# Local transformers on 32-query blocks: values stationary in 64x64 tiles, probabilities divided in SBUF by DVE, mask laid by products of 64 rows, values moved tile by tile

## The reference, cut to what matters

```python
WINDOW, HEADS, DIM_HEAD, DEPTH = 32, 16, 64, 6
x = shift_tokens(x)                      # channels 64.. come from the token before
q, k, v = split(x @ Wqkv)                # 16 heads of 64
q = rotary(l2norm(q) * qs); k = rotary(l2norm(k) * ksc)
sim  = einsum('bhwie,bhwje->bhwij', bq, bk2) * 8.0   # bq: blocks of 32 queries,
                                                     # bk2: the 32 keys before and the 32 own
sim  = where((i < j) | (i > j + 32) | (j == -1), -max, sim)
out  = einsum('bhwij,bhwje->bhwie', softmax(sim), bv2)
x    = x + out @ Wo
h    = layernorm(shift_tokens(x)) @ W1 + b1          # then a * gelu(gate) @ W2 + b2, added to x
```

## Time and profile before

| | |
|---|---|
| median of 3 runs | 4340.34 us (4339.49 to 4340.35) |
| span of the profiled execution | 4339.8 us |
| first local transformer, first projection to end | from about 505 us to 2145 us |
| one iteration in the steady stretch | 32.65 us (1502.14 to 1534.79) |
| iterations in the two local transformers | 2 x 48 and their tails |
| mean granted TensorE clock | 0.957, in the steady stretch 1.00 |

### The profile page before, as it was taken

One profiled execution on the slowest core, in us unless ns is written; L12 is line 12 of the kernel. 1 busy time (PEld: TensorE's weight loads), 2 busy tenths in 40 slices (PEclk: granted clock), 3 DMA queues, 4 the chain that ended last, 5 costly groups with the idle time before them and its releaser, 6 DMA issues. The chain is left out here.

```text
span 4339.8 us, 130231 instructions
## 1 busy us (share of the span) xinstructions
PE 3995.2 (92%) x46283; PEld 2655.5 (61%) x46283; DVE 3715.0 (86%) x12505; ACT 3380.3 (78%) x10657; POOL 3380.2 (78%) x4196
## 2 busy tenths in 40 slices
PE   6888799999999999999767999999999999996686
PEld 2333357767767767766553677767776776763464
DVE  6999789999999999999476999999999999974646
ACT  5888489999999999999414999999999999983122
POOL 3999698888888888888296888888888888861313
PEclk7999899999999999999897999999999999997887
DMA  1000101111111111111002111111111111100000
GB/s 28 1 1 1 46 24 31 41 31 36 41 27 49 31 34 44 26 34 27 15 1 53 31 27 41 36 41 31 36 41 27 51 29 29 37 24 3 6 3 10
DMA packets 78571, 122.04 MB, mean 28 GB/s; under 512 B 26024, under 2 KB 47204, under 8 KB 77924
## 3 DMA queue, kind: packets, MB, share of 16 engines
q1 hardware_dynamic: 77924, 113.71, 10.3%
HBM read 35.56 MB, written 1.05 MB: 8 GB/s over the span
## 5 line engine op out<-in xcount | busy, mean ns | idle before, releaser
L1095 POOL TENSOR_TENSOR local_qk<-local_qk,local_rb 128x512 f32<-128x512 f32 x768 | 975.7, 1271 | 224.2 <-DVE local_rb L1485 210.1
L1365 ACT ACTIVATE local_pr<-local_tb,local_nmax 128x96 f32<-128x96 f32 x3072 | 995.0, 362 | 68.7 <-DVE local_nmax L1501 67.1
L1191 PE MATMUL local_pj<-local_wqkv,local_xs 128*128 128x512 f32 x1536 | 808.4, 619 | 31.8 <-DVE local_rb L1485 17.8
L1101 POOL TENSOR_TENSOR local_qk<-local_qk,local_rinv 128x512 f32<-128x512 f32 x768 | 786.6, 1045 | 7.5
L1501 DVE CUSTOM_DVE_ANT_0 local_tb<-local_tb,local_mask 128x96 f32<-128x96 f32 x3072 | 689.2, 290 | 46.5 <-PE local_tb L1213 43.7
L1365 ACT ACTIVATION_READ_ACCUMULATOR local_pr<-local_tb,local_nmax 128x1 f32 x3072 | 703.3, 229 | 0.0
L1117 POOL TENSOR_TENSOR local_pr<-local_pr,local_rsum 128x384 f32<-128x384 f32 x768 | 622.4, 826 | 36.5 <-DVE local_rsum L1507 36.5
L1482 DVE TENSOR_TENSOR local_qk<-local_pj,local_rope 128x512 f32<-128x512 f32 x768 | 523.6, 682 | 62.8 <-ACT local_sq L1348 44.1
L1348 ACT ACTIVATE local_sq<-local_pj 128x512 f32<-128x512 f32 x768 | 462.2, 627 | 123.3 <-PE local_pj L1191 119.0
L1485 DVE TENSOR_TENSOR local_rb<-local_pj,local_rope 128x512 f32<-128x512 f32 x768 | 523.2, 681 | 2.8 <-POOL local_qk L1095 2.8
L1492 DVE TENSOR_REDUCE local_ss<-local_sq 128x8 f32<-128x512 f32 x768 | 512.0, 678 | 2.6 <-ACT local_sq L1348 0.8
(11 more groups left out here) (425 smaller groups left out, 7954.8 us busy)
## 6 DMA issues: line engine op xcount, KB each, us to landing
local_v<-local_v SPq DMA_DIRECT2D x288, 256.0 KB, 3.9
local_wqkv<-L_ffn_Wqkv_dram SPq DMA_DIRECT2D x72, 256.0 KB, 4.7
local_wo<-L_ffn_Wo_dram SPq DMA_DIRECT2D x12, 512.0 KB, 4.0
local_w<-L_ffn_W_dram SPq DMA_DIRECT2D x12, 341.0 KB, 4.8
mamba_parts<-mamba_in_low SPq DMA_DIRECT2D x24, 64.0 KB, 2.0
local_w<-L_ffn_W_dram SPq DMA_DIRECT2D x12, 128.0 KB
y_dram<-store_xtok SPq DMA_DIRECT2D x4, 256.0 KB, 2.9
local_oT<-rope_dram SPq DMA_DIRECT2D x2, 256.0 KB, 2.7
```

The lines of the kernel that those rows point to most:

```text
L1095: nc.gpsimd.tensor_tensor(qk[:, u, :], qk[:, u, :], rb[:, u % 2, :], ALU.add).then_inc(s["summed"], 1)
L1101: nc.gpsimd.tensor_tensor(heads8(qk[:, u, :]), heads8(qk[:, u, :]), r, ALU.mult).then_inc(s["scaled"], 1)
L1191: nc.tensor.matmul(bank[:, :], xs[:, par, u // 4 * P:(u // 4 + 1) * P], wqkv[:, dep % 2, u % 4 * BANK:(u % 4 + 1) * BANK], start=True, sto ...
L1365: ins = nc.scalar.activation(pr[:, (NU * c + k) % PR_RING, i, WIN:WIN + KW], scores[:, i * KW:(i + 1) * KW], ACT.Exp, scale=-1.0, bias=nma ...
```

## The change

The local transformer is rewritten around blocks of 32 queries. Number of parts per seq, before and after:

- `score`: 2 tiles of 128 tokens in place of 4 couples. Per tile 64 matmuls with 64x32 stationary and 64x64 moving, in eight tiles of the array (two halves of the rows, four quarters of the columns): 128 matmuls per seq in place of 64.
- `lay_mask` is new: per tile two bfloat16 products of 64 rows put the mask into the score banks before the scores are added to it. `maxima` becomes 4 plain reductions of 128x512 in place of 32 custom instructions.
- `exps`: 4 x 8 instructions of 128x64 in place of 8 x 4 of 128x96.
- the division moves from POOL (`norm_p`) to DVE (`scale_p`, 4 of 128x512).
- `turn_probs`, `copy_probs`: half as many (2 and 4).
- `weigh`: 64 matmuls per tile with 64x64 stationary and 64x32 moving, in four tiles of the array: 128 per seq in place of 64. Output in a pair of `tb`, no longer in a bank of its own; `copy_o` goes to ACT, `copy_v` to DVE.
- `move_v`: 6 DMAs for tile 0 and 8 for tile 1, of 64 KB and 128 KB, in place of 3 of 256 KB.
- the stream is kept skewed (channels 64.. one column on), so `shift_in` and the second copy in `residual1` go; `out_project` and `down` write the two halves of the channels by separate matmuls of 128x64 stationary and 257 columns.
- the inverse root of the layer norm's variance joins the one of q and k on POOL (two more columns in `root`, `spread_root` in place of ACT's `spread_std`), the ten `std` steps on DVE go. `root` of seq a serves the layer norm of seq a-3 (`ROOT_LEAD`).
- the FFN has two banks, `fa` and `fb`; b2 becomes a row of W2.
- each seq's chain is one iteration shorter (`TAIL` 4 in place of 6; the first part's lags are all 0).
- `normalise` of a local transformer writes its result by halves (8 instructions in place of 4).

```diff
-QB = 64
+QB = 32
 KW = QB + WIN
-PR_RING = 6
-PT_RING = 2
+PR_RING = 3
-TAIL = 6
+TAIL = 4
...
-                for i in range(4):
-                    for h, low in ((0, 0), (1, 1), (0, 1), (1, 0)):
-                        own, p, q = slice(h * DH, (h + 1) * DH), 4 * half + i, QB * (2 * t + low)
-                        ins = nc.tensor.matmul(sc[h][low * QB:(low + 1) * QB, i * KW:(i + 1) * KW], qT[own, par, p, q:q + QB],
-                                               kT[own, par, p, q:q + KW], start=True, stop=True)
+                for p in range(PAIRS):
+                    for i in range(BLOCKS):
+                        for h in range(2):
+                            own, q = slice(h * DH, (h + 1) * DH), t * P + i * QB
+                            ins = nc.tensor.matmul(sc[h][i * QB:(i + 1) * QB, p * KW:(p + 1) * KW], qT[own, par, p, q:q + QB],
+                                                   kT[own, par, p, q:q + KW], start=False, stop=True, skip_group_check=True)
...
+            def lay_mask(c, par, t):
...
+                for h in range(2):
+                    rows = slice(h * HALF, (h + 1) * HALF)
+                    nc.tensor.matmul(sc[h][:, :], owner[rows, t, :], view(maskb[rows, 0:1], [[0, PAIRS], [1, KW]]), start=True, stop=True)
...
+                for i in range(BLOCKS):
+                    for p in range(PAIRS):
+                        for h in range(2):
+                            col, at = (h + p) % 2 * DH, p * HALF + i % 2 * QB
+                            ins = nc.tensor.matmul(ob[h][col:col + DH, p // 2 * P + i * QB:p // 2 * P + (i + 1) * QB],
+                                                   window(par, BLOCKS * t + i, h)[:, p, :], prT[h * KW:(h + 1) * KW, t, i // 2, at:at + QB],
+                                                   start=True, stop=True)
...
-                for i in range(4):
-                    at = scores[:, i * KW:(i + 1) * KW]
-                    ins = nc.vector.tensor_tensor_reduce(at, at, mask[:, k // 4, :], -1.0, 3.0e38, ALU.add, ALU.min, nmax[:, k, i:i + 1])
+                nc.vector.tensor_reduce(nmax[:, t, h, :], pair_of_banks("score", t)[h][:, :].rearrange("p (a k) -> p a k", k=KW),
+                                        AX.X, ALU.max, negate=True).then_inc(s["maxed"], 1)
...
+            def scale_p(c, par, k):
...
+                nc.vector.tensor_tensor(own, own, view(rsum[:, t, h, 0:1], [[1, PAIRS], [0, KW]]), ALU.mult).then_inc(s["p_scaled"], 1)
...
+                for h in range(2):
+                    row, other = h * HALF, (1 - h) * HALF
+                    sp.dma_start(vw[row + QB:row + 2 * QB, par, 4 + t, :, :], v[0:QB, par, t, h, :, :]).then_inc(moved, 16)
+                    if t:
+                        sp.dma_start(vw[row:row + QB, par, 5, :, :], v[3 * QB:P, par, 0, h, :, :]).then_inc(moved, 16)
+                    sp.dma_start(vw[row:row + HALF, par, t, :, :], v[other:other + HALF, par, t, h, :, :]).then_inc(moved, 16)
+                    sp.dma_start(vw[row:row + HALF, par, 2 + t, :, :], v[QB:3 * QB, par, t, h, :, :]).then_inc(moved, 16)
...
+                for j in range(4 * part, 4 * part + 4):
+                    for h in range(2):
+                        own = slice(h * HALF, (h + 1) * HALF)
+                        ins = nc.tensor.matmul(fa[own, 0:L + 1], wo[:, j, own], oT[:, j, 1 - h:L + 2 - h], start=(j == 0), stop=(j == INNER // P - 1),
+                                               skip_group_check=True)
```

More of the change, by code:

```diff
@@ L1086, in _ @@
             for i in range(2):
[L1087 removed]
+                for t in range(TILES):
+                    sp.wait_ge(s[f"v_moved{i}{t}"], MOVES[t] * SEQS // 2)
         @block.gpsimd
@@ L1269, in variance @@
                 for t in range(2):
-                    ins = nc.tensor.matmul(fb[:, L + t:L + t + 1], sq2[:, t * P:(t + 1) * P], net.mean[:, :], start=True, stop=True)
+                    ins = nc.tensor.matmul(fb[:, L + t:L + t + 1], work[:, t * P:(t + 1) * P], net.mean[:, :], start=True, stop=True)
                 ins.then_inc(s["var_ready"], 1)
@@ L1275, in spread @@
                 pe.wait_ge(s["diag_ready"], e + 1)
-                for t in range(2):
-                    ins = nc.tensor.matmul(fb[:, t * P:(t + 1) * P], net.ones[:, :], diag[:, t, :], start=True, stop=True)
-                ins.then_inc(s["spread"], 1)
+                nc.tensor.matmul(fb[:, L:2 * L], net.ones[:, :], work[:, :], start=True, stop=True).then_inc(s["spread"], 1)
             def up(e, par, part):
@@ L1333, in iteration @@
                 run(out_project, 3, 1)
-                run(project, 0, 3)
-                run(turn_qk, 1, 1)
-                run(turn_probs, 2, 1)
-                run(weigh, 2, 0)
-                run(score, 1, 0)
+                run(project, 0, 5)
+                run(project, 0, 6)
+                run(centre, 3, 0)
+                run(turn_qk, 1, 3)
+                run(weigh, 2, 0)
+                run(project, 0, 7)
+                run(variance, 3, 0)
+                run(turn_probs, 2, 1)
@@ L1340, in _ @@
+                run(lay_mask, 1, 1)
+                run(project_v, 0, 0)
+                run(score, 1, 1)
+                run(weigh, 2, 1)
+                run(project_v, 0, 1)
+                run(project_v, 0, 2)
+                run(project_v, 0, 3)
             pipeline(pe, iteration)
@@ new lines, in iteration @@
+                run(bias_xn, 4, 0)
+                run(copy_o, 3, 3)
+                run(square, 0, 0)
+                run(square, 0, 1)
+                run(copy_qk, 1, 0)
+                run(copy_qk, 1, 1)
+                run(gelu, 4, 0)
+                run(square, 0, 2)
+                run(gelu, 4, 1)
+                run(gelu, 4, 2)
+                run(copy_probs, 2, 0)
+                run(copy_qk, 1, 2)
+                run(copy_qk, 1, 3)
+                run(copy_probs, 2, 1)
+                run(copy_qk, 1, 4)
@@ new lines, in iteration @@
+                run(square, 0, 3)
+                run(square, 0, 4)
+                run(copy_qk, 1, 5)
+                run(exps, 1, 0)
+                run(exps, 1, 1)
+                run(square, 0, 5)
+                run(square2, 3, 0)
+                run(copy_qk, 1, 6)
+                run(square, 0, 6)
+                run(copy_qk, 1, 7)
+                run(copy_o, 2, 0)
+                run(copy_o, 2, 1)
+                run(square, 0, 7)
+                run(copy_probs, 2, 2)
+                run(copy_probs, 2, 3)
@@ L1573, in residual2 @@
                     dve.wait_ge(s["z_ready"], B + f + 1)
-                    nc.vector.tensor_tensor(net.xT[:, f % B, :], net.xT[:, f % B, :], z[:, f % B, :], ALU.add)
+                    for own, first in ((slice(0, HALF), 0), (slice(HALF, P), 1)):
+                        nc.vector.tensor_tensor(net.xT[own, f % B, :], net.xT[own, f % B, :], stream[own, f % B, first:first + L], ALU.add)
             def iteration(run):
-                run(rotate, 1, 0)
-                run(recip, 3, 2)
-                run(maxima, 3, 7)
@@ L1619, in iteration @@
-                run(maxima, 2, 4)
+                run(recip, 2, 1)
                 run(gate, 4, 1)
+                run(sum_squares, 0, 1)
+                run(sum_squares, 0, 2)
                 run(gate, 4, 2)
-                run(maxima, 2, 5)
-                run(recip, 2, 1)
-                run(copy_o, 3, 3)
-                run(residual2, 4, 0)
-                run(maxima, 2, 6)
+                run(maxima, 1, 0)
+                run(maxima, 1, 1)
+                run(rotate, 0, 3)
+                run(scale_p, 2, 2)
@@ L1628, in _ @@
+                run(scale_p, 1, 0)
+                run(maxima, 1, 2)
+                run(maxima, 1, 3)
+                run(copy_v, 0, 0)
+                run(copy_v, 0, 1)
+                run(scale_p, 1, 1)
+                run(copy_v, 0, 2)
+                run(copy_v, 0, 3)
             dve.sem_inc(s["z_ready"], B)
```

653 lines of the change are left out of this document (277 added, 376 removed).

## The result

The changed kernel took 4529.0 us (median of four, 4519.5 to 4531.7) against 4340.35 of before: a ratio of 1.043 (95% interval 1.041 to 1.044). The forecast was 4250 us, with a range up to 4460. So it was slower where faster was forecast, and outside the range.

What follows compares the result with a forecast made beforehand. PE's matmul stream was taken as the bound: blocks 28.7, block changes 2.7 and waits 0.3 made 31.7 us an iteration against 32.65. Over 88 iterations, with end and layer norm, that gave 4250 us, range 4165 to 4460.

Steps and rivals of the forecast that it cites:

- a score row: PE's score, 256 instructions an iteration in eight tiles: 10 ns each, 2.6 us in all, against 2.8 before.
- a values' row: PE's weigh, 256 instructions an iteration in four tiles: 3.7 us, if four weight loads run beside each other.
- the output projection: On PE, with down, twice the matmuls at half width: 4.8 us together if halves run side by side, 4.8 more otherwise.
- Rival B: Small matmuls on PE start no faster than 25 to 26 ns apart: iteration 38.5 us, 4845 us in all; chance 0.12.
- rival C: Weigh's loads in four tiles do not run beside each other: weigh 5.3 or 7.4 us, total 4385 or 4575; chance 0.17.
- I add 0.3 for waits: Last term of PE's iteration: 0.3 us for waits on top of 31.4, giving 31.7 us.
- the chains in the prediction: POOL's root, second projection's rotation, probabilities of tile 1 and last rotation: each ready before PE wants it, nearest by 0.7 us.
- Rival D: PE's stream falls to 31.4 us, but a tight chain or unfreed bank costs 1 us an iteration: about 4335; chance 0.13.
- Eight waves of 96 x 0.84 ns: Price of a score block before the change, 32 scores in waves of four tiles: put at 0.69 us.
- its own range of 4165 to 4325: The forecast's range without rivals, from score at 1.7 to 3.4 us and weigh at 2.6 to 4.2 us an iteration.
- The moves: The 14 DMAs of values, 8.3 us of SP's queue in an iteration of 31.7: costed at nothing.
- start, end and layer norm: Per transformer: start unchanged, end 6 us shorter, layer-norm writes 2.5 us longer.

Runs made afterwards that it cites:

- experiments 2: Changed kernel with three long rows of small matmuls added ahead of each local transformer's first iteration; time not compared, 3.65 us mean between groups in the first row.
- 3: Changed kernel with 122 fulfilled waits added per iteration on PE's queue, in two versions with instruction pieces cut at different places: 5001 us and 4930 us.
- 5: Changed kernel with two projections between second score row and values' row (the rows apart), and copy_v's wait relaxed: 4322 us, 0.9951 of before.
- 7: Changed kernel with half of the values' matmuls of tile 1 left out, so output is not the reference's: 4331 us.
- experiment 1: Changed kernel with each of the 14 DMAs that move values carrying one partition only, output not the reference's: 4532 us, 1.044 of before.

## Why the prediction was wrong

**What bounds the kernel, and the steady iteration: right.** An undisturbed iteration is 31.57 us for 31.7 forecast. Term by term, from start to start: a score row 1.42 (11 ns an instruction; taken: 10), a values' row 1.86 without the change of block (taken: 1.86), so the loads of four tiles do run beside each other; the output projection 3.57 (taken 3.45 with a column more), so the halves run side by side; down 1.36. No engine beside PE became the bound. Rival B (25 ns a start) and rival C (slower weight loads) both named a slower row of small matmuls, and both are refuted as mechanisms by the same rows, since inside a piece the matmuls go at 11 and 14.5 ns. That the result lies near C's 4575 is chance.

**The step that failed is "I add 0.3 for waits".** I multiplied a row's pace by its count and took the result as the row's time, with 0.3 us an iteration for everything else. It was 3.06 us (34.63 - 31.57):
- 2.17 us of pauses inside rows of small matmuls (93.5 us over 43 iterations), for instructions that were still being fetched (experiments 2, 3, 5 and 7);
- 0.5 to 0.7 us of slower clock. It stood at 0.50 for 58 us of the stretch from 605 to 2050, and in the kernel before for none of it. Set beside the same blocks of the undisturbed iteration, the blocks in that time are 22 us longer without their pauses (41 iterations), 0.54 an iteration; 0.7 is all that is left of the 3.06. In these stretches it fell only in kernels with pauses, and it is back at 1.00 in the kernel with the rows apart;
- 0.17 us of waits for copied values (7.3 us), the chain through `copy_v`. It was not one of the chains in the prediction.

Put into the sum: 88 x (34.6 - 31.7) = 255 us on top of 4250 is 4505 us, for 4529 measured. Rival D had the shape of the result (waits take the place of the gain), but named data chains as the mechanism and 1 us as the price. None of the chains that it listed (POOL's root, the probabilities of tile 1, the rotations) shows up in PE's waits of the steady stretch of the changed kernel.

Two sums in the prediction are off and changed nothing. Eight waves of 96 x 0.84 ns are 0.64 us, not 0.69. And its own range of 4165 to 4325 doesn't follow from its bounds: score and weigh both at their low ends would be 88 x 2.0 = 176 us less, 4074, and both at their high ends 114 us more, 4364.

**Could it be seen before?** Partly. The page of before lists 370 fetches of 16 KB on the instruction queue, and the stretch of the earlier trace rows has 456 matmuls and 460 loads in 32.65 us: a piece of 256 lasts 9 us on the mean, and the first six blocks of the earlier trace rows hold 220 instructions (110 matmuls and their loads) in 6.8 us. That view gives no latency, since no fetch was ever waited for. But after the change the same count is 256 instructions in 1.4 us, six times denser than the mean before, and that was in my own sum, where I take 10 ns for each of them. A resource that is used six times as hard in places and whose limit isn't known belongs in the range with an upper end of its own; mine had none.

**Moves, POOL, start and end.** The moves are free (experiment 1). POOL's new product and the shorter chain cost nothing that the waits show. The excess of the 45 or so steady iterations in each transformer (some 2 us over the 32.65 of before) is about 90 of its 95 us, so start, end and layer norm came out within a few us of even, for 3.5 us of gain forecast.

## What to carry to other kernels

Count instructions per microsecond as well as work per microsecond, over the densest stretch and not on the mean: an unrolled stream is fetched in pieces, and in this kernel a piece of 256 instructions that PE uses up in the middle of a dense stretch cost some 3.45 us (3.1 to 4.1), however fast its matmuls were. When small matmuls are cut smaller, put matmuls of many columns between the rows, so that any 256 instructions in a row last long enough; look first for the wait that such a move runs into, and move no more than the one row that holds most of the pauses. Idle time put down to issue in the middle of a row whose data are there is the sign to look for, and so are iterations of one code that differ in length.

## What the runs showed of the hardware

- An instruction fetch is 16 KB and takes mostly 0.9 to 1.5 us. In a row of small matmuls the next piece is usable 3.45, 3.73 or 4.0 us after PE crossed into the one before (a mean of 3.65 in the added row). It makes 28.5 ns for each small matmul in a long row of score's shape, while within a piece they go at 10 to 11 ns (64x32 stationary, 64 columns, eight tiles) and 14.5 ns (64x64, 32 columns, four tiles).
- With pauses of 1.4 to 2 us in a dense row PE's clock fell from 2.4 to 1.2 GHz in part of the time: a group of 128 took 1.48 us, then 2.05. In the changed kernel the mean clock over the first transformer's steady stretch was 0.98, with the rows apart it was 1.00.
- A wait on PE's queue that is already fulfilled costs some 0.1 us once the queue ahead of it has run dry (106 of them: 10.95 us). With 122 in an iteration it was 37.8 us long, where the undisturbed one is 31.57 and the changed kernel's mean 34.63.
- Iterations of identical code ran from 31.57 to 37.08 us, since an iteration of 1414 instructions is 5.5 pieces and its rows meet the cuts in another place each time.
